# Mixture-of-experts stage of a decoder block: slices of 256 slots, and seven slices of 128

## The reference

```python
x = layernorm(x + gated_conv(x))            # w_in, causal conv of 4 taps, silu gates, w_out
x = layernorm(x + cross_attention(x, ctx))  # 16 heads
x = layernorm(x + ffn(x))

# ffn, with E = 8 experts, TOP_K = 2, D = 512, DE = 352, DS = 704
shared = silu(x @ Ws_gate) * (x @ Ws_up) @ Ws_down
scores = softmax(x @ W_router)              # 8 per token
topk_vals, topk_idx = top_k(scores, 2)
h = silu(x @ We_gate[e]) * (x @ We_up[e])   # for each expert e, 352 wide
routed = sum over the two chosen e of topk_vals * (h @ We_down[e])
out = routed + shared
```

## Time and profile before

| | us |
|---|---|
| median of 3 runs | 1124.37 |
| the profiled execution's own time | 1129.32 |
| its span, from the first to the last instruction | 1127.0 |
| granted TensorE clock, mean over the span | 0.973 |
| stage `experts`, from its first matmul on PE to its last | 645.4 to 966.2 |

### The profile page before, as it was taken

How to read it: one execution, slowest core, us unless ns; L and a number is a source line. 1 busy time by engine, 2 the same in 40 slices (tenths; PEclk the granted TensorE clock), 3 DMA queues, 4 the chain that set the end, 5 groups by cost and what they waited for, 6 DMA issues and landing times. The chain is left out here.

```text
span 1127.0 us, 19172 instructions
## 1 busy us (share of the span) xinstructions
PE 1066.7 (95%) x6774; PEld 905.1 (80%) x6774; DVE 691.8 (61%) x1533; ACT 456.9 (41%) x810; POOL 275.8 (24%) x368
## 2 busy tenths in 40 slices
PE   7899999999889999998679799999999999899997
PEld 6688888888678888877558599999999999777785
DVE  4836466474467767764537566777677776253576
ACT  5614334154245445544333245555555555221210
POOL 4510100121323333334242122222222221323030
PEclk9999999999969999999989899999999999999999
DMA  5403050215958788874231376666666764524142
GB/s 168 168 1 112 0 195 0 70 43 162 211 171 211 211 231 231 218 189 152 71 126 52 121 252 230 226 232 228 228 231 235 235 229 158 168 75 133 53 149 75
DMA packets 88628, 176.20 MB, mean 156 GB/s; under 512 B 8224, under 2 KB 36128, under 8 KB 86784
## 3 DMA queue, kind: packets, MB, share of 16 engines
q1 hardware_dynamic: 81904, 151.91, 43.2%
q0 software_dynamic: 6672, 23.60, 6.3%
HBM read 132.75 MB, written 39.32 MB: 153 GB/s over the span
## 5 line engine op out<-in xcount | busy, mean ns | idle before, releaser
L45 PE MATMUL e_ps_h<-e_x_lo,e_gu_hi 128*128 128x256 f32 (+1 forms) x552 | 158.0, 286 | 2.9 <-DVE e_x_lo L1972 2.6
L47 PE MATMUL e_ps_h<-e_x_hi,e_gu_hi 128*128 128x256 f32 (+1 forms) x552 | 155.8, 282 | 0.0
L46 PE MATMUL e_ps_h<-e_x_hi,e_gu_lo 128*128 128x256 f32 (+1 forms) x552 | 155.5, 282 | 0.0
L45 PE MATMUL a_ps_proj<-region_a_rounded,arena 128*128 128x512 f32 x272 | 107.8, 396 | 9.9 <-DVE region_a_rounded L369 6.2
L953 DVE CUSTOM_DVE_ANT_0 b_dump<-b_ps_s,b_mask 128x128 f32<-128x128 f32 (+1 forms) x256 | 80.4, 354 | 48.7 <-PE b_ps_s L1143 45.3
L46 PE MATMUL a_ps_proj<-region_a_rounded,arena 128*128 128x512 f32 x272 | 107.0, 393 | 0.0
L47 PE MATMUL a_ps_proj<-region_a_rounded,arena 128*128 128x512 f32 x272 | 106.8, 393 | 0.0
L45 PEld LDWEIGHTS e_ps_h<-e_x_lo,e_gu_hi 128*128 128x128 f32 (+1 forms) x552 | 100.5, 182 | 4.6 <-DVE e_gu_lo L1976 3.4
L46 PEld LDWEIGHTS e_ps_h<-e_x_hi,e_gu_lo 128*128 128x128 f32 (+1 forms) x552 | 100.1, 181 | 1.0
L47 PEld LDWEIGHTS e_ps_h<-e_x_hi,e_gu_hi 128*128 128x128 f32 (+1 forms) x552 | 100.0, 181 | 0.0
L388 DVE SCALAR_TENSOR_TENSOR f_region_b<-a_ps_proj,a_taps,f_region_b 128x510 f32<-128x510 f32 (+2 forms) x96 | 71.7, 747 | 41.3 <-ACT f_region_b L328 39.1
(11 more groups left out here) (353 smaller groups left out, 2705.8 us busy)
## 6 DMA issues: line engine op xcount, KB each, us to landing
f_region_a<-we_gate_up SPq DMA_DIRECT2D x88, 352.0 KB, 5.1
qk_split<-arena SPq DMA_DIRECT2D x24, 512.0 KB, 5.7
f_region_a<-we_down SPq DMA_DIRECT2D x23, 512.0 KB, 6.8
y_slots<-f_region_b SPq DMA_DIRECT2D x23, 512.0 KB, 2.8
f_x_next<-x SPq DMA_DIRECT2D x7, 1024.0 KB, 5.6
b_sk<-qk_split SPq DMA_DIRECT2D x24, 256.0 KB, 4.2
b_sq<-qk_split SPq DMA_DIRECT2D x24, 256.0 KB, 5.9
region_b_rounded<-qk_split SPq DMA_DIRECT2D x18, 256.0 KB, 4.3
```

The costliest lines, as they stand in the source:

```text
L45: pe.matmul(out, a_hi, b_lo, start=first, stop=False)
L46: pe.matmul(out, a_lo, b_hi, start=False, stop=False)
L47: return pe.matmul(out, a_hi, b_hi, start=False, stop=last)
```

## The change

The experts' work is cut into 16 slices of 256 slots and 7 of 128, 4992 slots in all. They come in the order large, large, small, seven times, and then large, large. Each expert's count is rounded up to blocks of 128 slots: whole pairs of blocks go to large slices, an odd block to a small one (with a rule for overflow into unused large slices). Slots of large slices come first in DRAM, those of the small ones behind them. The loop's body holds six slices (three turns), and five slices stand after it.

In a small slice the 128 tokens are stationary and the weights move: gate and up are 4 chunks x 3 passes = 12 matmuls of 352 columns each, into one PSUM bank each. The hidden values come out with tokens on partitions, so they are turned by three transposes (`small_turn`) before `down`. PE computes the first unit of the next slice inside the small slice, in two halves around `small_turn`.

```diff
 SLOTS = 256
-E_TILES = (2 * T + E_N * (SLOTS - 1)) // SLOTS
 BLOCKS = SLOTS // P
-NB = E_TILES * BLOCKS
+PAIRS = 2 * T // SLOTS
+SINGLES = E_N - 1
+E_TILES = PAIRS + SINGLES
+SPAN = 3
+NB = BLOCKS * PAIRS + SINGLES + 1
...
+            def small_hidden(m, k, s):
+                p = k % 2
+                cols = slice(s * DE, (s + 1) * DE)
+                for c in range(DC):
+                    if s == 0:
+                        wait_inputs(m, k, c)
+                    mm = three_pass(pe, bank(s), x_hi[:, p, c, 0:P], x_lo[:, p, c, 0:P],
+                                    gu_hi[:, p, c, cols], gu_lo[:, p, c, cols], c == 0, c == DC - 1)
                 mm.then_inc(h_ready, 1)
...
+            def small_turn(m, k):
+                pe.wait_ge(h_done, count(m, k, U, 1) + 1)
+                for u, n in enumerate(E_UNITS):
+                    mm = pe.transpose(ps_t[0:n, u], small_hf[:, u * P:u * P + n], ident[:])
+                mm.then_inc(h_ready, 1)
+
+            def small_down(m, k):
+                pe.wait_ge(dn_lo_done, number(m, k) + 1)
+                pe.wait_ge(y_read, count(m, k, BLOCKS, 1))
+                pe.wait_ge(h_lo_done, count(m, k, U, 1) + 1)
+                for u, n in enumerate(E_UNITS):
+                    mm = three_pass(pe, ps_y[:, 0], small_hi[0:n, u], small_lo[0:n, u], dn_hi[0:n, u], dn_lo[0:n, u],
+                                    u == 0, u == U - 1)
+                mm.then_inc(y_ready, 1)
...
+            def large_tile(m, k):
+                if k % SPAN == 1:
+                    hidden(m, k, 0)
+                    turn(m, k + 1)
+                hidden(m, k, 1)
+                if k % SPAN == 0:
+                    turn(m, k + 1)
+                hidden(m, k, 2)
+                for units in ((0, 1), (2,)):
                     for b in range(BLOCKS):
-                        down(i, b, u)
+                        down(m, k, b, units)
+
+            def small_tile(m, k):
+                small_hidden(m, k, 0)
+                turn(m, k + 1)
+                small_hidden(m, k, 1)
+                pe.wait_ge(silu_done, count(m, k, U, 1) + 1)
+                hidden(m, k + 1, 0, (0,))
+                small_turn(m, k)
+                hidden(m, k + 1, 0, (1,))
+                small_down(m, k)
```

ACT in the new order. The second output block of a large slice is copied out by ACT, no longer by DVE; three of the four chunks of the slice behind the small one are split at the end of the large slice ahead of it:

```diff
+            def large_tile(m, k):
+                if k % SPAN == 1:
+                    split_down(m, k)
+                gate(m, k, 0)
+                split_gate_up(m, k + 1, 0)
+                if k % SPAN == 0:
+                    split_down(m, k)
+                round_hidden(m, k, 0)
+                split_gate_up(m, k + 1, 1)
+                gate(m, k, 1)
+                split_gate_up(m, k + 1, 2)
+                round_hidden(m, k, 1)
+                split_gate_up(m, k + 1, 3)
+                split_x(m, k + 1)
+                gate(m, k, 2)
+                round_hidden(m, k, 2)
+                if k % SPAN == 1:
+                    for c in range(3):
+                        split_gate_up(m, k + 2, c)
+                output(m, k)
+
+            def small_tile(m, k):
+                split_down(m, k)
+                split_gate_up(m, k + 1, 3)
+                act.wait_ge(h_ready, U * number(m, k) + 1)
+                act.activation(small_sg, bank(0), ACT.Silu).then_inc(silu_done, 1)
+                split_x(m, k + 1)
+                act.wait_ge(h_ready, U * number(m, k) + 3)
+                last = E_UNITS[2]
+                act.activation(small_hi[:, 0:2], ps_t[:, 0:2], ACT.Copy)
+                act.activation(small_hi[0:last, 2], ps_t[0:last, 2], ACT.Copy).then_inc(h_hi_done, 1)
```

DVE has the same order in a large slice (with the copy of the first output block at its end). In a small one:

```diff
+            def small_tile(m, k):
+                split_gate_up(m, k + 1, 3)
+                split_x(m, k + 1)
+                dve.wait_ge(silu_done, count(m, k, U, 1) + 1)
+                dve.wait_ge(h_ready, U * number(m, k) + 2)
+                dve.tensor_tensor(small_hf[:], bank(1), small_sg, ALU.mult).then_inc(h_done, 1)
+                split_down(m, k)
+                dve.wait_ge(h_hi_done, count(m, k, U, 1) + 1)
+                last = E_UNITS[2]
+                dve.tensor_tensor(small_lo[:, 0:2], ps_t[:, 0:2], small_hi[:, 0:2].bitcast(F32), ALU.subtract)
+                dve.tensor_tensor(small_lo[0:last, 2], ps_t[0:last, 2], small_hi[0:last, 2].bitcast(F32), ALU.subtract)\
+                    .then_inc(h_lo_done, 1)
+                output(m, k)
```

SP's queue. The down weights now have two raw buffers (the second in a region that is free in this stage):

```diff
+            def tile(m, k):
+                every = range(DC)
+                if k % SPAN == 0:
+                    load_gate_up(m, k + 2, every[:1])
+                    load_down_of(m, k + 2)
+                    load_gate_up(m, k + 2, every[1:])
+                if k % SPAN == 1:
+                    load_down_of(m, k + 2)
+                    load_gate_up(m, k + 2, every)
+                    load_gate_up(m, k + 3, every[:3])
+                if small(k):
+                    load_gate_up(m, k + 2, every[3:])
+                    load_down_of(m, k + 2)
+                store(m, k)
```

In `route` the slots are counted by blocks. The chain of links on eight or sixteen numbers per partition is longer, `expert_of` is computed later, between the parts of `shared.up` (now `product` and `rest`), and the first `shared.add` stands ahead of the multiplication by token numbers:

```diff
-            link(dve.tensor_scalar(tiles_i[:], run[:, :, NT - 1], float(SLOTS - 1), None, ALU.add))
-            link(dve.tensor_scalar(tiles_i[:], tiles_i[:], SLOTS.bit_length() - 1, None, ALU.logical_shift_right))
+            link(dve.tensor_scalar(rows_i[:], run[:, :, NT - 1], float(P - 1), None, ALU.add))
+            link(dve.tensor_scalar(tiles_i[:, 0], rows_i[:], SLOTS.bit_length() - 1, None, ALU.logical_shift_right))
+            link(dve.tensor_scalar(tiles_i[:, 1], rows_i[:], P.bit_length() - 1, 1, ALU.logical_shift_right, ALU.bitwise_and))
             link(dve.tensor_copy(tiles_f[:], tiles_i[:]))
...
+            link(dve.tensor_scalar(odd_base[:], first[:, 1], twice[:], float(P), ALU.add, ALU.mult))
+            link(dve.tensor_scalar(spill[:], first[:, 1], all_pairs, float(SLOTS), ALU.add, ALU.mult))
...
             link(dve.tensor_tensor(pos[:], prior, tot[:].rearrange("p e t -> p t e"), ALU.add))
+            link(dve.tensor_tensor(cand[:], pos[:], of_experts(limit[:]), ALU.is_ge))
+            link(dve.tensor_tensor(cand[:], cand[:], of_experts(odd_base[:]), ALU.mult))
+            link(dve.tensor_tensor(pos[:], pos[:], of_experts(pair_base[:]), ALU.add))
+            link(dve.tensor_tensor(pos[:], pos[:], cand[:], ALU.add))
...
             link(dve.tensor_tensor(hot_lo[:], repeat(col128[:], P), spread(part_f[:, 1], P), ALU.is_equal))
             link(dve.tensor_tensor(hot_hi[:], repeat(col_nb[:], NB), spread(part_f[:, 0], NB), ALU.is_equal))
+            dve.wait_ge(x2_stored, 16)
+            shared.add(dve, kept, 0, 0)
             for k in range(2):
                 rows = hot_hi[:, k * NT:(k + 1) * NT]
...
-            dve.wait_ge(x2_stored, 16)
-            for t in range(TILES):
+            for t in range(1, TILES):
```

More of the change, by code:

```diff
@@ L1410, in up @@
             .then_inc(self.h_lo_done, 1)
+    def up(self, dve, n, u):
+        self.product(dve, n, u)
+        self.rest(dve, n, u)
     def down(self, pe, n, t):
@@ L1861, in _ @@
         def _(sp):
[L1862 to L1868, removed]
-            def load_down_of(i):
-                at = slice(i, i + 1) if isinstance(i, int) else bass.ds(i, 1)
-                e = sp.value_load(rt.expert_of[0:1, at], min_val=0, max_val=E_N - 1)
-                sp.wait_ge(dn_lo_done, i)
-                load_down(sp, e, w_down, raw, dn_loaded)
@@ L1928, in gate, with split_x @@
-            def gate(i, u):
+            def split_x(m, k):
+                if exists(m, k):
+                    done = count(m, k, HALVES, 1)
+                    if small(k):
+                        act.wait_ge(x_ready, done + 1)
+                        act.activation(x_hi[:, k % 2, :, 0:P], ps_x[:].rearrange("p a c n -> p (a c) n")[:, :, 0:P], ACT.Copy)\
+                            .then_inc(x_hi_done, 1)
+                    else:
+                        for a in range(HALVES):
+                            act.wait_ge(x_ready, done + a + 1)
+                            act.activation(x_hi[:, k % 2, a * HC2:(a + 1) * HC2], ps_x[:, a], ACT.Copy).then_inc(x_hi_done, 1)
@@ new lines, in tile @@
+            def tile(m, k):
+                if small(k):
+                    small_tile(m, k)
+                else:
+                    large_tile(m, k)
+            split_gate_up(0, 0, 0)
+            split_x(0, 0)
+            for c in range(1, DC):
+                split_gate_up(0, 0, c)
+            act.wait_ge(carried, 1)
+            with act.Fori(0, TURNS) as m:
+                for k in range(BODY):
+                    tile(m, k)
+            for k in range(TAIL):
+                tile(TURNS, k)
@@ L2030, in _, with tile @@
+            def tile(m, k):
+                if small(k):
+                    small_tile(m, k)
+                else:
+                    large_tile(m, k)
+            split_gate_up(0, 0, 0)
+            split_x(0, 0)
+            for c in range(1, DC):
+                split_gate_up(0, 0, c)
+            with dve.Fori(0, TURNS) as m:
+                for k in range(BODY):
```

(14 more changed lines are left out.)

423 lines of the change are left out of this document (244 added, 179 removed).

## The result

The changed kernel ran in 1088.88 us (median of four, 1086.77 to 1095.80) against 1124.55 before: ratio 0.9686, 95% interval [0.9638, 0.9733]. The forecast was 1083, its range 1071 to 1100.

The account below looks back on a forecast made before the run. PE's instructions were taken to bound `experts`: seven triples going from 41.46 to 35.4 us save 42.4, route adds 1.2, so 1129.3 - 41.2 = 1088.1 profiled, less 4.95 gives a median of 1083 us, range 1071 to 1100.

Parts of the forecast that it names:

- What bounds the kernel: In the steady part of `experts`, PE is busy 289.79 of 290.20 us, so the stage costs what PE's instructions cost.
- The work on PE: PE's matmuls and transposes in three slices (large, large, small): 33.91 us without waits, 352-column matmuls at 0.161 each.
- Rival 1: No waits to speak of in `experts`: chunks land sooner, a triple costs 33.9 us, the kernel 1073; chance 0.17.
- The waits: PE's idle time in one triple of slices: 1.0 + 0.3 + 0.2 = 1.5 us, bounds 0 and 3.9, making 35.4.
- the tokens: In the small slice PE waits 1.0 us for the first half of the next slice's split tokens.
- the last unit's rest: In the large slice behind the small one, PE waits 0.2 us for the last hidden unit's rest.
- `down` of the small slice: PE waits 0.3 us ahead of it for DVE's rests of the turned hidden values.
- Route: The stage ahead of `experts`: a longer chain on DVE, less the moved add, delays everything after by 1.2 us; bounds 0, +3.
- The offset: Median runs taken to stand 4.95 us below the profiled execution: 1088.1 profiled becomes 1083.
- Rival 2: The small slice loses more: loads landing at 7.5 us give 1100, or a clock fall after PE's wait 1094; chance 0.17.
- Rival 3: Each of the loop's two jumps back waits for code: 1087 us, up to 1091 with ACT and DVE; chance 0.06.
- Rival 4: Slower than before: the single raw buffer paces `experts` once landings pass 11.6 us; at 12.5 the kernel takes 1143; chance 0.03.

Follow-up runs that it names:

- all_three: Changed kernel with down weights split after tokens and loaded after chunks, and token splitting moved around the last hidden unit's steps: 1071.68 us, ratio 0.9536 to before.
- add_back: Changed kernel with the shared FFN's first add put back behind the multiplication by token numbers: 1091.28 us, ratio 0.9700 to the kernel before.

## Why the prediction was right, and where it was not

- **What bounds the kernel**: right. The time went with PE's instructions.
- **The work on PE**: right to 1%. 352 columns cost 0.162 where 0.161 was taken from the line through 256 and 512; three slices without waits were put at 33.91, and in `all_three` most cost 33.73, in which PE has no idle stretch. Rival 1 is this floor, reached by another order and not by this one.
- **The formula of the Trainium skill** ("TensorE: Matmul & The Clock Gate", section "Back-to-back issue gap") would have put 352 columns at 149 ns; measured are 162. Its remark that a stream of loads and matmuls is spaced by both agrees with the 111 ns of 128 columns, but the figure that it gives for such a stream there, some 81 ns, is lower; the measurement decides.
- **The waits**: the place and the cause were right, the sizes were not. A triple cost 35.85 where the sum had 35.4, and the terms moved both ways. Counted from start to start against a triple of `all_three` without waits (33.73), the tokens cost 1.4 per triple and not 1.0, and the last unit's rest 0.7 and not 0.2, which is the largest miss. `down` of the small slice was given 0.3; the two intervals around its first matmul are 0.2 longer than elsewhere, with no idle stretch, and that is so in `all_three` too, so it is part of the 33.73. The remaining 0.1 is spread over many matmuls. Two steps were mis-sized. One is the landing, for which I took the median of 5.1: in the densest stretch of the triple the chunk stands behind 704 KB and beside 512 KB of tokens and took up to 7.35. So the idle time for tokens is not one number but 0 to 2.25 (over the seven small slices 8.3 / 7 = 1.2). The other is what a wait costs: I counted it as idle time, and it costs some 0.26 more. Six triples saved 33.6 us of the 36.4 expected; the part ahead of the first small slice 0.4 of 0.7, and the last three slices 4.3 of 5.4.
- **Route**: +1.2 forecast, +0.3 measured. One link of the chain was carried over at a duration that it no longer has. It is the first of the two on the slot's parts; in the kernel before and in the changed one:

```profile
613.62 1.22 DVE L1715 TENSOR_SCALAR r_part_i<-f_slot 128x32 int32<-128x32 int32 x1
```

```profile
619.34 0.18 DVE L1776 TENSOR_SCALAR r_part_i<-f_slot 128x32 int32<-128x32 int32 x1
```

  That is 1.0 us. Why it took 1.22 stays open; the move of the add gave what was expected.
- **The offset**: the profiled execution was forecast at 1088.1 and took 1088.47, but the median at 1083, by carrying over that the median lay 4.95 below the profile. For the changed kernel the two differ by 0.4, so that was no property to carry over. Where those 4.95 lay is not fully shown, since there is one trace of the kernel before: its first product of `route`, at 592.34, lies some 1.3 us behind the middle of the twelve traces (591.0), which is part of it. Part of the agreement is luck: the stage gave 4.1 us less than forecast, `route` took 0.9 less, scatter ahead of it gave 1.9, and what lies behind the stage 0.9.
- **Rival 2**, the larger loss: its first half is what happened, in small. Its second half, a fall of the clock, did not happen in `experts` in this trace: a wait of 2.25 us left it at 1.00, that is 2.4 GHz. That was luck: in `add_back` it fell to 0.51 (1.2 GHz) behind a wait of 1.99 in a small slice, and in `route` of the changed kernel, behind the 1.85 ahead of the third `down`, it was 0.53 from 626.7 to 629.0. The length of the wait alone does not tell which it will be.
- **Rival 3**: no cost of the jumps that shows. **Rival 4**: the landing never neared the 11.6 us from which it decides.

## What to carry to other kernels

Where slices are padded to a whole tile, a smaller tile pays less where its matmuls run into the cost of loading the stationary operand (24 us here in place of 38): with few rows, make the rows stationary and let the weights move. When a phase is shortened, ask which transfers now fall into one burst, and size their landing by what is queued with them, not by the median; what is needed last goes last into the queue, and long splits that nobody waits for go behind short ones that PE waits for. Count what a wait of PE costs from start to start, not as idle time. Compare stages between the traces, not spans, when unchanged code scatters by more than the effect.

## What had not been expected of the hardware

- With a stationary operand of 128 x 128, matmuls of 128 columns start 0.111 us apart and those of 256 0.117; with 128 x 96 and 128 columns, 0.085.
- PE's clock stayed at 1.00 through a wait of 2.25 us between busy stretches, where it had fallen to 0.52 after one of 2.90. The length of the gap alone does not decide: in cross attention, in the kernel before, the clock was 0.57 in the 3.6 us behind a wait of 1.70.
- The same chunk of 352 KB landed in 2.9 to 7.5 us within one execution (median 4.7), and the length of the same triple of slices moved with it from 34.67 to 37.09 us.
